# Attention of an adaLN transformer block: both heads of a pair side by side in 64-row tiles, in blocks of two key tiles

## What is computed

```python
h = _layernorm(x, axis=-1) * (1 + ca) + sa
qkv = X @ W_qkv + b_qkv                       # X is h here
qkv = qkv.reshape(b, l, H, 3 * DK).transpose(0, 2, 1, 3)
Q, K, V = jnp.split(qkv, 3, axis=-1)
scores = jnp.einsum('bhqd,bhkd->bhqk', Q, K) / np.sqrt(DK).astype(np.float32)
attn = jax.nn.softmax(scores, axis=-1)
out = jnp.einsum('bhqk,bhkv->bhqv', attn, V)
out = out.transpose(0, 2, 1, 3).reshape(b, l, H * DK)
return out @ W_fc + b_fc
```

## Time and profile before

| | |
|---|---|
| time, median of 3 runs | 1919.57 us (1918.49 to 1923.9) |
| the profiled execution | 1924.27 us, span 1922.4 us |
| mean granted clock of PE | 0.972 |
| attention, first projection to last `attnT` | 43 to 1695 us of the span |

### The profile page before, as it was taken

How to read it: one execution, slowest core, us unless ns; L and a number is a source line. 1 busy time by engine, 2 the same in 40 slices (tenths; PEclk the granted TensorE clock), 3 DMA queues, 4 the chain that set the end, 5 groups by cost and what they waited for, 6 DMA issues and landing times. The chain is left out here.

```text
span 1922.4 us, 28484 instructions
## 1 busy us (share of the span) xinstructions
PE 1818.5 (95%) x7819; PEld 985.9 (51%) x7819; DVE 1455.9 (76%) x2303; ACT 1080.1 (56%) x2008; POOL 1163.7 (61%) x521
## 2 busy tenths in 40 slices
PE   4899999999999999999999999999999999946996
PEld 3444555555555554555455555555455555434886
DVE  5677777777777777777777777777777777677788
ACT  4455555555555555555555555555556555424874
POOL 4465666776666666667666666666776666711124
PEclk8899999999999999999999999999999999966999
DMA  2111111111111111111111111111111112000010
GB/s 84 50 38 34 39 34 36 35 38 38 38 38 38 31 34 37 29 37 38 38 38 38 38 33 38 38 33 33 38 38 38 38 38 67 1 22 22 25 37 28
DMA packets 51520, 70.63 MB, mean 37 GB/s; under 512 B 6269, under 2 KB 29338, under 8 KB 51482
## 3 DMA queue, kind: packets, MB, share of 16 engines
q1 hardware_dynamic: 51328, 70.15, 13.1%
q10 hardware_dynamic: 154, 0.03, 0.0%
HBM read 14.58 MB, written 2.10 MB: 9 GB/s over the span
## 5 line engine op out<-in xcount | busy, mean ns | idle before, releaser
L552 POOL TENSOR_TENSOR ACC<-ACC,PR 128x1024 f32<-128x1024 f32 x382 | 925.5, 2423 | 217.8 <-ACT PR L614 207.8
L614 ACT ACTIVATE PR<-ps_s 128x512 f32<-128x512 f32 x1024 | 555.3, 595 | 568.1 <-PE ps_s L815 562.3
L646 DVE TENSOR_REDUCE NM<-ps_mx 128x1 f32<-128x1024 f32 x508 | 616.5, 1214 | 180.2 <-PE ps_mx L800 174.8
L824 PE MATMUL ps_o<-PR,V 128*64 128x512 f32 x2048 | 550.7, 616 | 0.0
L814 PE MATMUL ps_s<-QA,KA 128*128 128x512 f32 x1024 | 459.0, 448 | 0.0
L815 PE MATMUL ps_s<-QB,KB 128*128 128x512 f32 x1024 | 405.9, 396 | 0.0
L814 PEld LDWEIGHTS ps_s<-QA,KA 128*128 128x128 f32 x1024 | 192.2, 188 | 401.6 <-issue 243.6
L552 POOL TENSOR_TENSOR ACC<-PR 128x1024 f32<-128x1024 f32 x64 | 155.5, 2429 | 330.0 <-ACT PR L614 330.0
L800 PE MATMUL ps_mx<-KA,QA 128*128 128x512 f32 x1016 | 327.3, 403 | 11.1 <-DVE NM L646 10.9
L678 DVE RECIPROCAL SUM<-SUM 128x128 f32<-128x128 f32 x256 | 241.3, 945 | 20.5 <-ACT SUM L591 18.7
L800 PEld LDWEIGHTS ps_mx<-KA,QA 128*128 128x128 f32 x1016 | 186.1, 189 | 75.2 <-DVE NM L646 34.8
(11 more groups left out here) (187 smaller groups left out, 1583.5 us busy)
## 6 DMA issues: line engine op xcount, KB each, us to landing
hcur<-hT SPq DMA_DIRECT2D x32, 512.0 KB, 2.9
KA<-KA SPq DMA_DIRECT2D x128, 128.0 KB, 2.3
QB<-QA SPq DMA_DIRECT2D x128, 128.0 KB, 2.3
Wraw<-in_L_attn_W_qkv SPq DMA_DIRECT2D x32, 192.0 KB, 2.4
x<-in_L_attn_X SPq DMA_DIRECT2D x4, 512.0 KB, 5.5
Wfc<-in_L_attn_W_fc SPq DMA_DIRECT2D x32, 64.0 KB, 1.8
hT<-in_L_attn_X SPq DMA_DIRECT2D x4, 512.0 KB, 5.8
out<-e_res SPq DMA_DIRECT2D x7, 256.0 KB, 2.3
```

Source lines behind the costliest of these rows:

```text
L552: G.tensor_tensor(ACC[:, ch, :, :], a, PR[:, t, :, :], ALU.add).then_inc(added, 1)
L614: A.activation(PR[:, t, h, :], ps_s[:, h, :], ACT.Exp, scale=SCALE).then_inc(exp_done, 1)
L646: D.tensor_reduce(NM[:, ch, h, i:i + 1], banks[:, :, :].rearrange("p a b -> p (a b)"), AX, ALU.max, negate=True).then_inc(mx_red, 1)
L824: last = T.matmul(ps_o[half(h), ch, :], V[:, u, t, half(h)], PR[:, t, h, :], start=(t == 0), stop=(t == 7))
```

## The change

The parts of Q and K are each one tensor with both heads of the pair on the 128 rows, 64 rows for a head: `QHI`, `QLO`, `KHI`, `KLO`. A matmul for one head uses 64 rows of the array and the two heads' matmuls are issued one behind the other, into different banks. The scores of a step are four such pairs (high by high, high by low, low by high, and the negative maxima `QN` through a matrix of ones and zeros `ONE`), 8 matmuls in place of 4. The maxima use the high parts alone, and a group is 128 queries by 512 keys for both heads (`max_both_heads`), in place of 1024 keys for one head; a small reduction joins the halves (`join_maxima`). The copies by DMA are gone.

The 16 steps become 8 blocks `b` of two. A block has its units, one group of maxima, the scores of both steps, the second group of maxima, and both products with V. The scores have four banks, two for each step, and the exponents of a step are one instruction. The units have no banks of their own: they use those of the scores at the start of a block, and PE waits until they have been read out (`read_out`) before it writes scores there. ACT writes the high part straight from the projection, and DVE the low part from the projection, the bias and the high part. DVE takes the output straight from `ps_o`. The product with V is in its own block, not one step later.

```diff
             return ctx.enter_context(nc.semaphore(name))
 
 
-        QA = sb("QA", [P, 2, 2, L], F32R)
-        QB = sb("QB", [P, 2, 2, L], F32R)
-        KA = sb("KA", [P, 2, 2, L], F32R)
-        KB = sb("KB", [P, 2, 2, L], F32R)
+        QHI = sb("QHI", [P, 2, L], F32R)
+        QLO = sb("QLO", [P, 2, L], F32R)
+        KHI = sb("KHI", [P, 2, L], F32R)
+        KLO = sb("KLO", [P, 2, L], F32R)
+        QN = sb("QN", [P, 2, 512], F32R)
+        ONE = sb("ONE", [P, P], F32R)
...
+        UNITS = {0: (("rows", 0, 0, 0), ("v", 1, 0, 1), ("fc", -1, 0, 2)),
+                 2: (("k", 1, 0, 0), ("k", 1, 1, 2), ("q", 1, 0, 3)),
+                 4: (("rows", 0, 1, 0), ("fc", -1, 1, 2)),
+                 6: (("q", 1, 1, 0), ("v", 1, 1, 2))}
+        SUMS = {0: (-1, 1), 4: (0, 0)}
+        SUMS_BANK = 3
+
+        INVERT = {(1, 0): (-1, 1, 0), (1, 1): (-1, 1, 1), (2, 0): (-1, 1, 2), (2, 1): (-1, 1, 3), (3, 0): (-1, 1, "O"),
+                  (5, 0): (0, 0, 0), (5, 1): (0, 0, 1), (6, 0): (0, 0, 2), (6, 1): (0, 0, 3), (7, 0): (0, 0, "O")}
...
+        FIRST_UNITS = (("k", 0, ps_s[:, 0, :]), ("k", 1, ps_s[:, 1, :]), ("q", 0, ps_s[:, 2, :]), ("q", 1, ps_s[:, 3, :]),
+                       ("v", 0, ps_o[:, 0, :]), ("v", 1, ps_o[:, 1, :]))
...
             def unit(kind, m, u, ch, ps_w):
                 q = slice(ch * 512, ch * 512 + 512)
                 if kind in "qk":
...
-                    A.activation(raw[:, ch, :], ps_w, ACT.Identity, bias=bias[:, u, ty:ty + 1]).then_inc(raw_in, 1)
-                    act.wait_ge(raw_in, raw_count(kind, m, ch))
-                    for h in range(2):
-                        last = A.activation(X[half(h), u, h, q], raw[half(h), ch, :], ACT.Copy)
-                    last.then_inc(hi, 1)
+                    A.activation(X[:, u, q], ps_w, ACT.Identity, bias=bias[:, u, ty:ty + 1]).then_inc(hi, 1)
...
+            def exponents(n, s):
+                ch, t = divmod(s, 8)
+                chunk = 2 * n + ch
+                wait(act, pv_done, 16 * n + s - 7)
+                wait(act, added, 7 * (chunk - 1) + max(t, 1))
+                act.wait_ge(scored, 16 * n + s + 1)
+                i = 2 * (t % 2)
+                A.activation(PR[:, t, :, :], ps_s[:, i:i + 2, :], ACT.Exp, scale=SCALE).then_inc(exp_done, 1)
...
+                for b in range(8):
+                    for kind, m, v, ch, bank in units_of(n, u, b):
+                        unit(kind, m, v, ch, ps_s[:, bank, :])
+                    exponents(n, 2 * b)
+                    exponents(n, 2 * b + 1)
+                    if b == 0 and has(n + 1):
+                        split_w(n + 1, 1 - u)
+                    if b in SUMS and has(n + SUMS[b][0]):
+                        copy_sums(n + SUMS[b][0], SUMS[b][1])
...
+            def reduce_max(m, u, ch, i, kc, count, banks=ps_mx[:, :, :]):
+
+                if i == 0 and kc == 0:
+                    wait(dve, nm_ready, 2 * m + ch - 1)
+                dve.wait_ge(mx_done, count + 1)
+                D.tensor_reduce(NMH[:, ch, i, kc, :], banks, AX, ALU.max, negate=True).then_inc(mx_red, 1)
+
+            def join_maxima(m, ch):
+
+                dve.wait_ge(mx_red, 8 * (2 * m + ch + 1))
+                wait(dve, rows_t, 2 * m + ch - 1)
+                D.tensor_reduce(NMW[:, ch, :, 0:4], NMH[:, ch, :, :, :].rearrange("p i k h -> p h i k"), AX,
+                                ALU.min).then_inc(nm_ready, 1)
...
+                if kind in "qk":
+                    HI, LO, ty, hi, lo = (KHI, KLO, 1, k_hi, k_lo) if kind == "k" else (QHI, QLO, 0, q_hi, q_lo)
+                    dve.wait_ge(hi, 2 * m + ch + 1)
+                    D.scalar_tensor_tensor(LO[:, u, q], ps_w, bias[:, u, ty:ty + 1], HI[:, u, q].bitcast(F32),
+                                           op0=ALU.add, op1=ALU.subtract).then_inc(lo, 1)
...
+                    D.tensor_tensor(QN[:, ch, :].rearrange("p (i q) -> p i q", i=4),
+                                    ps_w[:, 0:P].unsqueeze(1).to_broadcast([P, 4, P]),
+                                    mask[:, :].unsqueeze(2).to_broadcast([P, 4, P]), ALU.mult).then_inc(neg_rows, 1)
...
+                    D.tensor_tensor(O[:, :], ps_o[:, ch, :], SUM[:, :], ALU.mult).then_inc(o_norm, 1)
...
+                    pe.wait_ge(nm_ready, 2 * m + ch + 1)
+                    T.transpose(ps_w[:, 0:P], flat(NMW[:, ch, :, :]), g.ident[:, :]).then_inc(rows_t, 1)
...
+            def read_out(kind, m, ch):
+
+                pe.wait_ge({"k": k_lo, "q": q_lo, "v": v_copied, "rows": neg_rows, "fc": fc_added}[kind], 2 * m + ch + 1)
+
+            def sums(m, ch):
+                pe.wait_ge(added, 14 * m + 7 * ch + 7)
+                for h in range(2):
+                    last = T.matmul(ps_s[half(h), SUMS_BANK, :], g.ones[:, 0:64], ACC[:, ch, h, :], start=True, stop=True)
+                last.then_inc(sums_mm, 1)
...
                 wait(pe, mx_red, count - ahead)
                 q = ch * 512 + i * P
-                for kc in range(2):
-                    last = T.matmul(banks[:, kc, :], QA[:, u, h, q:q + P], KA[:, u, h, kc * 512:(kc + 1) * 512],
+                for h in range(2):
+                    last = T.matmul(banks[:, h, :], QHI[half(h), u, q:q + P], KHI[half(h), u, kc * 512:(kc + 1) * 512],
                                     start=True, stop=True)
                 last.then_inc(mx_done, 1)
...
                     pe.wait_ge(neg_rows, 2 * n + ch + 1)
-                    pe.wait_ge(qdup[u][ch], 32 * (n // 2) + 32)
+                    pe.wait_ge(q_lo, 2 * n + ch + 1)
                     if ch == 0:
                         pe.wait_ge(k_lo, 2 * n + 2)
+                i = 2 * (t % 2)
                 for h in range(2):
-                    wait(pe, exp_done, 32 * n + 2 * s + h - 1)
-                    T.matmul(ps_s[:, h, :], KA[:, u, h, k], QA[:, u, h, q], start=True, stop=False)
-                    T.matmul(ps_s[:, h, :], KB[:, u, h, k], QB[:, u, h, q], start=False, stop=True).then_inc(scored, 1)
+                    T.matmul(ps_s[:, i + h, :], KHI[half(h), u, k], QHI[half(h), u, q], start=True, stop=False)
+                for h in range(2):
+                    T.matmul(ps_s[:, i + h, :], KHI[half(h), u, k], QLO[half(h), u, q], start=False, stop=False)
+                for h in range(2):
+                    T.matmul(ps_s[:, i + h, :], KLO[half(h), u, k], QHI[half(h), u, q], start=False, stop=False)
+                for h in range(2):
+                    last = T.matmul(ps_s[:, i + h, :], ONE[half(h), :], QN[half(h), ch, :], start=False, stop=True)
+                last.then_inc(scored, 1)
...
+                for b in range(8):
+                    units = units_of(n, u, b)
+                    for kind, m, v, ch, bank in units:
+                        unit(kind, m, v, ch, ps_s[:, bank, :])
+                    group = maxima(n, u, b, 0)
+                    if group:
+                        max_both_heads(*group)
+                    for j in range(2):
+                        for kind, m, v, ch, bank in units:
+                            if bank // 2 == j:
+                                read_out(kind, m, ch)
+                        if j == 1 and b - 1 in SUMS and has(n + SUMS[b - 1][0]):
+                            pe.wait_ge(sums_in, 2 * (n + SUMS[b - 1][0]) + SUMS[b - 1][1] + 1)
+                        scores(n, u, 2 * b + j)
+                    group = maxima(n, u, b, 1)
+                    if group:
+                        max_both_heads(*group)
+                    times_v(n, u, 2 * b)
+                    times_v(n, u, 2 * b + 1)
+                    if b in SUMS and has(n + SUMS[b][0]):
+                        sums(n + SUMS[b][0], SUMS[b][1])
 
             def last():
-                times_v(NP - 1, 1, 15)
```

More of the change, by code:

```diff
@@ L435, in has, with units_of, maxima, first_banks @@
         def has(n):
             return not isinstance(n, int) or 0 <= n < NP
+        def units_of(n, u, b):
+            return [(kind, n + d, u if d == 0 else 1 - u, ch, bank) for kind, d, ch, bank in UNITS.get(b, ()) if has(n + d)]
+        def maxima(n, u, b, j):
+            if b < 4:
+                return (n, u, 1, b, j, 8 + 16 * n + 2 * b + j)
+            if has(n + 1):
+                return (n + 1, 1 - u, 0, b - 4, j, 8 + 16 * n + 2 * b + j)
+            return None
+        def first_banks(k):
+            return (ps_mx[:, :, :], ps_s[:, 0:2, :], ps_s[:, 2:4, :])[k % 3]
@@ L625, in last @@
             def last():
[L626 to L627 removed]
+                copy_sums(NP - 1, 1)
             run(act, pair, first, last)
@@ new lines, in first @@
+                for k in range(8):
+                    reduce_max(0, 0, 0, k // 2, k % 2, k, first_banks(k))
+                dve.wait_ge(s_init, 4)
+                dve.wait_ge(s_mask, 3)
+                join_maxima(0, 0)
+            def pair(n, u):
+                for b in range(8):
+                    for kind, m, v, ch, bank in units_of(n, u, b):
+                        unit(kind, m, v, ch, ps_s[:, bank, :])
```

(26 more changed lines are left out.)

292 lines of the change are left out of this document (67 added, 225 removed).

## The result

The changed kernel takes 1824.47 us (median of 4 runs, 1822.86 to 1831.29), the kernel before 1921.3 beside it: ratio 0.950, 95% interval 0.947 to 0.953. It is faster, inside the forecast's range, and 36 us above the forecast of 1788. The profiled execution took 1822.86, span 1821.4.

The account below looks back on a forecast made before the run. PE's instruction stream was taken as the limit. Blocks 8 x 4.5, units 9.4 and bank stalls 1.0 make 46.4 us a pair against 50.5, saving 127 over 31 pairs, plus 6 at the start: 1788 us, range 1745 to 1905.

Parts of the forecast that it names:

- p: On PE, distance between pairs of 64-row matmuls, one per head; taken as 0.24 us, the two running beside each other.
- The block without units: On PE, ten matmul pairs, two V products and form changes: 4.53 us, taken as 4.5, where two steps cost 5.22.
- the first part: Start of the kernel, from first projection to first exponent: 27.9 us falls to 21 to 24, 6 us taken off.
- block 6's stall: In block 6, which has a Q unit, PE waits 0.3 us for a bank to be read out.
- the wait of 0.3 for the reduction: In block 2, the second group of maxima waits 0.3 us more for DVE's first reduction.
- A change of form: On PE, switching between 64-row or 64-column matmuls and the whole array: 0.11 one way, 0.10 us back.
- Rivals (1) to (4): Dearer pairs of 64-row matmuls: 0.267 (chance 0.18), 0.29 (0.06), 0.36 (0.09), 0.46 (0.07) us; 1862, 1910 to 1925, 2072, 2310 us.
- with the small ones: DVE's work for a pair, listed operations plus unlisted small ones: some 35 us, so DVE stays under PE.
- The last line of the forecast: Signs of error: p, form changes dearer than 0.1 us, or DVE falling back in inversion blocks and holding up maxima.
- The gain of a pair: Attention, one pair of heads: 46.4 us against 50.5, 4.1 less, for 31 pairs 127 us.
- the forecast's own range: Whole kernel: 1750 (blocks of 4.4, no bank stalls) to 1835 us (blocks of 4.7, stalls doubled); chance 0.60.
- rival (1): Weight loads of 64-row matmuls go one by one: 0.267 us a pair, block 4.8, time 1862 us; chance 0.18.

Follow-up runs that it names:

- one_half: Changed kernel with head 1's score matmuls reading head 0's rows, so both heads use one row half; 2326.68 us, ratio 1.212.
- split_late: Changed kernel with the single instruction for the weights' low part moved on DVE from block 0 to block 1; 1762.48 us, ratio 0.919.
- max_one_head: Changed kernel with each group of maxima taken as 128 queries by 1024 keys of one head; 1881.50 us, ratio 0.981.
- head_by_head: Changed kernel with each step's four score matmuls of head 0 issued first, then head 1's four; 1872.29 us, ratio 0.974.
- exp_halves: Changed kernel with a step's exponent made in two instructions of 512 columns; 1870.04 us, ratio 0.975.

## Why the prediction came out as it did

**Right.** The price on which it all hung, p, was 0.23 for 0.24, read off the V product in the earlier trace rows; one_half shows that it is the two row halves that give it. The block without units took 4.47 for 4.5, the two long exponents 1.94 for 1.95, O 0.68 and the low part 0.75 for 0.70 each, the first part 5.8 us for 6, block 6's stall 0.40 for 0.3. In block 2 the scores of the second step came 0.46 late for 0.4 (800.76 to 802.15, less 0.93), but the wait of 0.3 for the reduction did not come. A change of form costs 0.11 (853.32 to 853.66, less 0.23). Rivals (1) to (4) all needed p of 0.267 or more and fell together. In the changed kernel, and in one_half too, a load runs beside its own half's matmul. By the sentence of the Trainium skill quoted in the forecast ("TensorE: Matmul & The Clock Gate", "Packing small matmuls") it should not; the trace disagrees, at 0.23 a start.

**Wrong: the step "with the small ones" of the account of DVE.** Among them was the weights' low part, for which the kernel before has 0.29 us twice in a pair. It took 2.15. I had counted DVE's busy time over a pair and found room for it, and had not asked what POOL does at the place to which `split_w` was moved, nor what is queued behind it: the reduction whose bank PE needs next. One wait of 1.77 us in 31 pairs is 55 us; split_late measures 62. The last line of the forecast named the effect, DVE falling back and holding up the maxima, but looked for it in the blocks with inversions.

The runs show that one of two instructions waits for the other's end (0.41 alone, 2.19 with its end 0.28 behind POOL's). The Trainium skill has this as a rule, in "SBUF — State Buffer", section "Who interferes with whom": a DVE instruction with two inputs in SBUF contends with a GpSimd instruction that reads SBUF, the shared port pair is "an exclusive lock", and the order of issue decides who is blocked. The trace agrees with it in both kernels (`Wlo` here, issued 0.44 behind POOL's addition, and L682 before, 1.12 for 0.69). It names instructions that stand in the diff, and had I gone through the moved ones by it, the term would have been bounded.

**Mis-sized the other way.** Without the collision the kernel takes 1763.9 in the profiled execution (split_late), 27 less than the forecast's 1791. The trace says where they are. The gain of a pair was taken too small by 0.56: a pair is then 46.0 for 46.4, and the pair before, taken from one distance as 50.5, has a mean of 50.7. With 63 chunks instead of 31 pairs that makes 147 us for the 127 (L769 from 65.6 to 1661.5 before, L709 from 60.7 to 1509.6 now). From the last `rows` to the last `attnT` it is 3.2 less (32.6 and 29.4), for which no gain was counted. And the part behind the attention, which the change doesn't touch, is 4.9 shorter in this run (228.3 and 223.4). The start gives back 1.1 less than the 6 counted. In the profiled executions the two errors are 59 too little for the collision (1822.9 less 1763.9) and 27 too much elsewhere, together the 32 by which 1791 missed. That they cancel in part is luck: with the rest as forecast, the collision alone would have made some 1847, above the 1835 that the forecast names as its own upper end.

**Slips in the sums.** 1791 less the 4.7 us is 1786, not 1788. The two ends of the forecast's own range do not follow from what is put beside them: blocks of 4.4 and no stalls are 1.8 us less for a pair, 56 less, 1732 and not 1750; blocks of 4.7 and doubled stalls are 2.6 more, 81 more, 1869 and not 1835. So the forecast's case and rival (1), at 1862, could not have been told apart by the time alone; the distance of 0.23 in the timeline does it.

## What to carry to other kernels

When an instruction of DVE that reads two operands from SBUF is moved, look at what GpSimd does at its new place, and then at what stands behind it on DVE: its price is a property of the place, and a busy time per pair doesn't show it. Two matmuls of 64 rows on different row halves cost as much as one, and the halves may be several instructions apart, so that work of one head can be put beside other work of the next; an imbalance is paid where something waits for both halves, here the exponent of both heads and the V product over all rows. When units share banks with the scores, count the work on PE between a unit's last matmul and the next write into its bank: here it must be 1.96 us.

## What was not expected of the hardware

- Matmuls start out of the program's order across row halves: one of the scores 0.33 us ahead of one of the maxima that stands before it (max_one_head), and the first matmul of head 1 together with the first of head 0, with three between them (head_by_head), the later ones about 0.11 behind. ACT's exponent, released by the increment on head 1's last matmul, still started only at the end of the later of the two last matmuls, 857.68 in max_one_head against 857.26 and 0.38.
- The granted clock of the attention is 1.00 in windows of the changed kernel, 0.98 in head_by_head, 0.98 to 0.99 in exp_halves and 0.96 to 0.97 in one_half: single dips, one of them to 0.86 from 890 to 915 us in one_half, where PE was busy 59.4 of the 61.6 us before. A pair with a dip takes 1.3 to 1.4 us more in head_by_head and exp_halves, and 3.1 in one_half. What sets them off stays open.
